# Expert scorer's attention pass: the slots of a step summed on VectorE, with the scan chain and the totals moved some steps back

## The reference, cut to what matters

```python
h = (x_flat @ W_gat).reshape(M, HEADS, NUM_EXPERTS)
a_src = (h * att_src).sum(-1)
a_dst = (h * att_dst).sum(-1)
e = jax.nn.leaky_relu(a_src[src] + a_dst[dst], negative_slope=0.2)
e_max = jax.ops.segment_max(e, dst, num_segments=M)
ee = jnp.exp(e - e_max[dst])
denom = jax.ops.segment_sum(ee, dst, num_segments=M)
alpha = ee / (denom[dst] + 1e-16)
agg = jax.ops.segment_sum(h[src] * alpha[:, :, None], dst, num_segments=M)
```

## Time and profile before

| what | value |
| --- | --- |
| time, median of 3 runs | 12754.23 us (12739.93 to 12757.21) |
| the profiled execution's own time | 12773.27 us |
| its span in the trace | 12771.6 us, granted TensorE clock 0.727 of full |
| PE, DVE, POOL, ACT busy in the span | 7698.0, 6064.4, 6049.9, 2359.1 us |
| the `be` pass, from its first gather to DVE's last instruction | 4396.66 to 5560.40 us |
| its gathers on POOL (L581) | 728, busy 699.4 us, idle before them 451.9 us |

### The profile page before, as it was taken

The page is one execution under the profiler, slowest core; times in us unless marked ns, Lnnn a source line. Parts: engine busy times, 40 slices in busy tenths (PEclk is TensorE's granted clock), DMA queues, the critical chain, the costliest instruction groups (busy, mean ns, idle before and its releaser), DMA issues. The chain is left out here.

```text
span 12771.6 us, 114013 instructions
## 1 busy us (share of the span) xinstructions
PE 7698.0 (60%) x32472; PEld 5982.8 (47%) x32472; DVE 6064.4 (47%) x17050; ACT 2359.1 (18%) x5596; POOL 6049.9 (47%) x6164
## 2 busy tenths in 40 slices
PE   4555464266664478835677575666746746666546
PEld 3334343255553377734566433445535635555334
DVE  6666665388886222232122244655651135444455
ACT  0122010011111144410122011133312211111001
POOL 0666556566662166605666405655521126666000
PEclk9666555577777677767788787777768967777777
DMA  1222122266665111213333602211343323336200
GB/s 46 61 61 64 37 83 63 61 183 183 184 180 92 24 19 19 19 49 90 92 91 92 68 7 50 46 42 43 41 42 105 103 57 96 95 95 90 32 4 22
DMA packets 478286, 903.72 MB, mean 71 GB/s; under 512 B 173139, under 2 KB 290029, under 8 KB 476915
## 3 DMA queue, kind: packets, MB, share of 16 engines
q0 software_dynamic: 277568, 621.62, 22.7%
q1 hardware_dynamic: 200106, 274.86, 6.7%
HBM read 827.17 MB, written 68.88 MB: 70 GB/s over the span
## 5 line engine op out<-in xcount | busy, mean ns | idle before, releaser
L581 POOL DMA_INDIRECT ee_rows<-e_table,net_mr_data x1000 | 998.2, 998 | 1118.9 <-POOLq L1725 466.6
L581 POOL DMA_INDIRECT ge_rows<-g_table,net_mr_data x1000 | 964.1, 964 | 652.1 <-issue 286.0
L913 POOL DMA_INDIRECT ce_rows<-c_table,net_mr_data x1000 | 950.8, 951 | 497.8 <-issue 236.9
L402 POOL DMA_INDIRECT main_slots<-em_load,em_where x784 | 817.2, 1042 | 637.1 <-DVE em_where L376 377.7
L581 POOL DMA_INDIRECT ae_rows<-a_table,net_mr_data x752 | 719.1, 956 | 411.2 <-issue 219.0
L581 POOL DMA_INDIRECT be_rows<-b_table,bx_br_data x728 | 699.4, 961 | 451.9 <-issue 196.3
L627 PE MATMUL ge_to_act<-ge_rows,net_eye 125*125 125x256 f32 x2000 | 636.9, 471 | 179.2 <-issue 172.0
L402 POOL DMA_INDIRECT gat_slots<-eg_load,eg_where x512 | 531.4, 1038 | 380.5 <-DVE eg_where L376 217.4
L627 PE MATMUL ee_to_act<-ee_message,net_eye 125*125 125x256 f32 x2000 | 570.4, 432 | 204.7 <-issue 202.1
L936 PE MATMUL ce_part_ps<-ce_rows,net_eye 125*125 125x256 f32 x2000 | 540.4, 417 | 190.9 <-DMA ce_rows<-c_table,net_mr_data 95.2
L359 PE MATMUL em_look_ps<-em_table,em_hot_tT 25*128 25x125 f32 x1568 | 319.9, 380 | 548.5 <-issue 328.3
(11 more groups left out here) (1006 smaller groups left out, 18294.0 us busy)
## 6 DMA issues: line engine op xcount, KB each, us to landing
em_key_row<-main_keys SPq DMA_DIRECT2D x98, 512.0 KB
f_w<-in_L_ffn_W_dram SPq DMA_DIRECT2D x40, 1024.0 KB, 11.8
eg_key_row<-gat_keys SPq DMA_DIRECT2D x64, 512.0 KB
ce_rows<-c_table,net_mr_data POOLq DMA_INDIRECT x1000
ee_rows<-e_table,net_mr_data POOLq DMA_INDIRECT x1000
ge_rows<-g_table,net_mr_data POOLq DMA_INDIRECT x1000
main_slots<-em_load,em_where POOLq DMA_INDIRECT x784
b_own_rows<-bx_kept SPq DMA_DIRECT2D x100, 125.0 KB
```

The costliest lines, as they stand in the source:

```text
L402: pool.indirect_dma_start(edge["slots"], bass.IndirectOffsetOnAxis(ap=where[:, c:c + 1], axis=0), load[:, c, :], None).then_inc(scattered, 16)
L581: pool.indirect_dma_start(rows[n][:, s, :], None, table, bass.IndirectOffsetOnAxis(ap=data[:, g, s, 0:1].bitcast(I32), axis=0)).then_inc(g ...
L913: pool.indirect_dma_start(rows[:, g % RING, s, :], None, table, bass.IndirectOffsetOnAxis(ap=data[:, g, s, 0:1].bitcast(I32), axis=0)).the ...
```

## The change

A new parameter `late` of `edge_pass`, set in the `be` call alone:

- `sum_slots` and `keep` are gone. In `send`, after a drain, DVE sums the 8 slots itself with one `reduce_sum` over a strided view, 16 sums of 8, written to `part`.
- POOL's wait before a step is on `message_ready` (raised by DVE in `send`) instead of `slot_summed`.
- The block chain and what follows run later: see `AT` in the diff. `total` is now at i-12, `scale` at i-11 and `add` at i-13, so that the loops have 6 more iterations (`END`). `hot` has 20 places and `part` 16.
- PE's order becomes flip, flip_back, own, turn, total, experts. `turn` uses one PSUM bank instead of two, and waits for the copy of the step before. `back_ps` has a bank of its own.
- `lent_part` is a new argument that no call uses.

```diff
-    HOTS, PARTS = 14, 8
+    HOTS, PARTS = (20, 16) if late else (14, 8)
+    AT = dict(flip=4, scan=5, flip_back=7, fall=9, factors=10, scale=11, total=12, lower=12, add=13) if late else dict(flip=3, scan=3, flip_back=4, fall=5, factors=5, scale=6, total=7, lower=6, add=7)
+    END = G + AT["add"] + 1
...
-        to_act = [ps(f"to_act{n}", [128, 512]) for n in range(2)]
+        to_act = [ps(f"to_act{n}", [128, 512]) for n in range(1 if late else 2)]
...
-        topT_ps = back_ps = ps("topT_ps", [128, 512])
+        topT_ps = ps("topT_ps", [128, 512])
+        back_ps = ps("back_ps", [128, 512]) if late else topT_ps
...
-                                pool.wait_ge(slot_summed, g - RING + 1)
+                                pool.wait_ge(message_ready if late else slot_summed, g - RING + 1)
...
                     pe.wait_ge(hot_ready, g + 1)
-                    if g >= 2:
+                    if late and g:
+                        pe.wait_ge(turned_sb, g)
+                    elif g >= 2:
                         pe.wait_ge(turned_sb, g - 1)
...
-                    if 0 <= i - 1 < G:
+                    if 0 <= i - 1 < G and not late:
                         sum_slots(i - 1)
-                    if QW and 0 <= i + 5 < G:
+                    if QW and 0 <= i + 5 < G and not late:
                         turn(i + 5)
                     if QW and 0 <= i + 3 < G:
                         own(i + 3)
+                    if QW and 0 <= i + 5 < G and late:
+                        turn(i + 5)
+                    if 0 <= i - AT["total"] < G and late:
+                        total(i - AT["total"])
...
-                    if 0 <= i - 2 < G:
+                    if 0 <= i - 2 < G and not late:
                         keep(i - 2)
...
+                    if late:
+                        dve.drain()
+                        sums = part[0:NP, g % PARTS, 0:W].rearrange("p (h v) -> p h v", h=H)[:, :, 0:dv]
+                        dve.reduce_sum(sums, values(g).rearrange("p s (h v) -> p h v s", h=H), axis=AX.X)
...
-            edge_pass(nc, edge, table, "add", 4, 4, 20, a_dst, 0.2, acc, const, "be", ring=8, tops=True, inner=inner)
+            edge_pass(nc, edge, table, "add", 4, 4, 20, a_dst, 0.2, acc, const, "be", ring=8, tops=True, inner=inner, late=True)
```

More of the change, by code:

```diff
@@ L499, with edge_pass @@
 BLOCK = 4
-def edge_pass(nc, edge, table, kind, H, dv, row_width, per_target, scores, acc, const, name, ring, more=(), lent=None, lent_whole=None, lent_top=None, tops=False, beside=None, inner=None):
+def edge_pass(nc, edge, table, kind, H, dv, row_width, per_target, scores, acc, const, name, ring, more=(), lent=None, lent_whole=None, lent_top=None, tops=False, beside=None, inner=None, late=False, lent_part=None):
     G, data, ids = edge["G"], edge["data"], edge["tile_of"]
@@ L532, in edge_pass @@
         message = sb("message", [128, 2, SLOTS, VW]) if kind == "mix" else None
-        part = sb("part", [128, PARTS, WA])
+        part = lent_part if lent_part is not None else sb("part", [128, PARTS, WA])
         bounds = lent if lent is not None else sb("bounds", [8, 4 * BLOCK * NP])
@@ L632, in flip @@
                     pe.wait_ge(topped, last + 1)
-                    if b:
+                    if b and late:
+                        pe.wait_ge(scanned, b)
+                    elif b:
                         pe.wait_ge(gap_ready, b)
@@ L642, in flip_back @@
                     pe.wait_ge(spread_ready, b + 1)
+                    if b and late:
+                        pe.wait_ge(gap_ready, b)
+                        pe.wait_ge(lowered, b)
                     for q in range(size[b]):
@@ L653, in total @@
                     ins.then_inc(totalled, 1)
-                for i in range(-5, G + 8):
-                    if 0 <= i - 7 < G:
-                        total(i - 7)
+                for i in range(-5, END):
+                    if 0 <= i - AT["total"] < G and not late:
+                        total(i - AT["total"])
                     for b in range(BLOCKS):
-                        if i == b * BLOCK + 3:
+                        if i == b * BLOCK + AT["flip"]:
                             flip(b)
-                        if i == b * BLOCK + 4:
+                        if i == b * BLOCK + AT["flip_back"]:
                             flip_back(b)
-                    if 0 <= i - 1 < G:
+                    if 0 <= i - 1 < G and not late:
                         sum_slots(i - 1)
-                    if QW and 0 <= i + 5 < G:
+                    if QW and 0 <= i + 5 < G and not late:
                         turn(i + 5)
@@ L684, in turned_copy @@
                     act.wait_ge(turned, g + 1)
-                    if 0 <= g - 6 < G:
+                    if 0 <= g - 6 < G and not late:
                         act.wait_ge(slot_summed, g - 5)
@@ L708, in factors @@
                         act.wait_ge(scaled, (b - 1) * BLOCK)
+                    if late and b * BLOCK + size[b] > PARTS:
+                        act.wait_ge(totalled, b * BLOCK + size[b] - PARTS)
                     if tops:
@@ L714, in factors @@
                     act.activation(fall[0:NP, b % 2, :], back_ps[0:NP, 64:64 + H], ACT.Exp).then_inc(lowered, 1)
-                for i in range(-6, G + 8):
+                for i in range(-6, END):
                     if 0 <= i + 1 < G:
@@ L821, in scale @@
                     dve.wait_ge(factor_ready, b + 1)
-                    dve.wait_ge(part_kept, g + 1)
+                    if not late:
+                        dve.wait_ge(part_kept, g + 1)
                     p = part[0:NP, g % PARTS, 0:W].rearrange("p (h v) -> p h v", h=H)
@@ L832, in _ @@
                 dve.memset(low[:, :], -FAR)
-                for i in range(-4, G + 8):
+                for i in range(-4, END):
                     if 0 <= i + 1 < G:
```

19 lines of the change are left out of this document (11 added, 8 removed).

## The result

The kernel after takes 12927.83 us (median of 4 runs, 12898.01 to 12929.96), the kernel before 12755.72 us (4 runs, 12739.93 to 12759.54). The ratio is 1.0132, with a 95% interval of 1.0114 to 1.0149: slower by 172 us. The prediction had the sign, and a third of the size (+55 us); the time lies above its range (12680 to 12890).

The account below looks back on a forecast made before the run. The bound was taken to be POOL's 10.0 us of gathers a step and their drain, with PE's signals late meanwhile. Steps +47, start -12 and end +20 made +55 us on 12754: 12809 us, range 12680 to 12890.

Parts of the forecast that it names:

- PE's work taken out is worth nothing: In `be`, leaving out PE records of 201.1 us, 2.2 a step, gains nothing, hidden by POOL and its drain.
- DVE's sum: In DVE's `send`, 0.3 us plus 0.1 for the drain a step, hidden; 36 us at most if uncovered.
- The start: Start of the `be` pass: step 8 may begin after DVE's message of step 0, 12 us earlier.
- POOL's wait: POOL's wait in `be`, moved from PE to DVE: steps of 12.3 instead of 11.73 us, +47 us over 82 steps.
- the forecast: The main case for `be`: steps of 11.9 to 13.5 us, 12776 to 12907 us; chance 0.47.
- The single bank: `turn` on PE waits for the copy of the step before, taken as made an iteration earlier: costs nothing.
- The end: From step 90 to the end of `be`: 117 us instead of 96, with 8 messages left, +20 us.
- The six added iterations: End of the `be` pass: six more iterations with only total, scale and add, 1 us each, 6 us.
- the signals come through: Rival: with DVE's gate PE's signals arrive freely, POOL takes 10.0 us a step; about -182, 12572 us; chance 0.17.
- The lock stays: Rival: POOL still pauses for the drain alone, 11.5 to 11.73 us a step; 12743 to 12762 us; chance 0.23.
- A mild gain: Rival: steps of 11.3 us in `be` or a shorter end, down to 12700 us; chance 0.10.
- DVE becomes the bound: Rival: DVE's added work in `be` is uncovered, 36 us, 12790 us; chance 0.03.

Follow-up runs that it names:

- both: Kernel after with `turn` behind the experts' matmuls and POOL waiting for PE again; 0.9985 and 1.0012 of before with pauses, 1.0014 on the chip without.
- turn_last_half: Kernel after with `turn` behind the experts' matmuls and POOL allowed 4 steps ahead instead of 8; 13031.63 us, 1.0147 of before.
- turn_last: Kernel after with `turn` behind the experts' matmuls, single bank kept; 12954.84 us, 1.0127 of before; on the chip without pauses 11660.33 us, 1.0012.
- pe_gate: Kernel after with POOL waiting for PE again, single bank kept; 12812.21 us, 1.0027 of before; on the chip without pauses 11715.87 us, 1.0058.
- before_one_bank: Kernel before with `turn` waiting for the previous step's copy, as with one bank; 1.0137 on the chip without pauses, 1.0070 on one with.
- the silent runs: Kernels before, after, and after with `turn` behind the experts' matmuls, without gathers past the first 8 steps; PE's ring 7.05, 10.32, 6.71 us a unit.

## Why the prediction was half right

- **What bounds the kernel** (PE's signals are late while POOL gathers, POOL's run and its silence make the step) held on every chip like that of the result. That it would not hold on all chips was not foreseen: on one of the five the signals are not late.
- **PE's work taken out is worth nothing:** right. "both" has all of it taken out, and DVE's sum in, and stands at 0.9985, 1.0012 and 1.0014.
- **DVE's sum:** 374 ns where I took 300. It is hidden, as said. By the Trainium skill ("VectorE: DVE Perf Modes", The TRN2 errata) it would be the 0.19 us estimated ahead, by a cost of which the same section says that it comes out too low for a single operation; the row has twice that.
- **The start:** step 8 begins 11.6 us earlier; predicted 12.
- **POOL's wait** (the gate): the mechanism is right, and it is the cause. With it undone alone, 1.0127 falls to 1.0027. The step that failed is the size of its term in the sum, "The ring of 8 is deeper than that of `ee` (5 places), so I take the row of 24 and the one of 64 as neighbours, and about 12.3". The length of a run isn't set by the ring's depth: turn_last_half has half of it and the same runs. It is set by how many messages PE's chain gets through, one in the silence and one soon behind it, and so no run without a stop of more than 0.3 us is longer than 16. The formula, (20 + 3 + 4.5) / 2 = 13.7 for runs of 16, stood in the prediction and met the measured 13.93 and 14.06 us of turn_last; it was fed the wrong length. Measured in the kernel after: 13.51 us, and +146 us over 82 steps instead of +47. That is just outside the 11.9 to 13.5 of the forecast, whose own range went to 12907 while the one stated stopped at 12890. The silence is put at "about 0.2 us a gather"; the three rows behind it give 0.21, 0.14 and 0.16, and the 2.75 us after 16 gathers 0.17.
- **The single bank, "nothing":** wrong as a price, and of little weight for this result. I had taken the copy as made an iteration earlier. It is made in the same one, behind Gelu and Exp on ACT's queue, and PE's ring goes from 7.05 to 10.32 us. With DVE's gate in place, the middle of the pass doesn't feel it: turn_last's steps are longer, not shorter. The end does: there the 8 messages that are left took 77 us (L806 starts at 5593.45 and 5670.56, the first five gaps between are 10.5 to 12.2 us) instead of the 64.5 predicted, and 58 in turn_last. The longer steps and the shorter end together leave turn_last at 12955 us, beside 12930. The six added iterations took 6.9 us from the last of the experts' results to the last add; predicted 6.
- **The rivals:** *the signals come through* is false where the result was measured and true on the one chip without pauses. There "both" and turn_last have steps of 10.1 us, but the kernel before is as fast (11645 us, 14 and 16 us less than the two), and the -182 us are not to be had. The Trainium skill's rule ("TensorE: Matmul & The Clock Gate", The cost: per-tile semaphore tail), some 26 ns for an increment, is nearer to the 0.08 us of that chip than to the others, where the signals wait up to 10 us behind the last gather. *The lock stays* is false for the kernel after, and is what pe_gate and "both" bring back. *A mild gain* and *DVE becomes the bound* are false: DVE is busy for 201.18 of 800 us.

**What stays open.** What holds PE's signals up, and why on most chips and not on one. It may be more than a signal: in the kernel before, while POOL issues its first 64 gathers, the four matmuls of one `own` (L617), with nothing but weight loads between them, come with wide gaps for which the profile names no wait (in the middle of the pass, at 4906.86, four of them take 0.85 us together):

```profile
4425.55 0.17 PE L617 MATMUL be_own_ps<-b_a_dst,be_hotT 125*125 x1
4426.21 0.17 PE L617 MATMUL be_own_ps<-b_a_dst,be_hotT 125*125 x1 [0.48 <-issue]
4429.01 0.17 PE L617 MATMUL be_own_ps<-b_a_dst,be_hotT 125*125 x1 [2.63 <-issue]
4431.11 0.17 PE L617 MATMUL be_own_ps<-b_a_dst,be_hotT 125*125 x1 [1.93 <-issue]
```

The chips differ in the gathers' transfers too. From 4450 to 4950 us the DMA engines are busy for a share of 0.49 in both2, on the chip without pauses, and of 0.15 in both3, at 22 and 18 GB/s; and DVE waits for gathered rows 91 times, 546.9 us in all, in both2, and once, 12.7 us, in both3. No run tells whether that is a cause or a consequence. Open is also what the kernel after costs on the chip without pauses: it never met it. before_one_bank (1.0137) and the silent runs (10.32 us against POOL's 10.0) let one expect a loss there too, from the bank; that is argued and not shown.

## What to carry to other kernels

Before you move a wait from a late signal to an early one, ask what the waiting engine's pauses were good for: here POOL's stop for PE was what let PE's signals through, and a gate on a third engine that is opened sooner made every cycle longer. Such a finding can hold on one chip and not on the next, so repeat the run on several before you settle on a mechanism. Size a stall that repeats itself by following one cycle to its end, each signal in turn, instead of by the depth of the buffer; the depth is only a limit. Where two buffers are made one, write down for each user of it what stands ahead on its engine's queue: the wait was on a copy of 0.35 us, the price was the Gelu and the Exp ahead of it, and with POOL silent an order with `turn` last paid nothing.

## What the runs showed of the hardware

- The same kernel takes 11645 us on one chip and 12777 to 12853 us on others. The difference is in POOL's idle time. For "both" on the first (both2) and on another (both3) the spans are 11654.2 and 12770.2 us, 1116 apart; POOL's idle time in its seven largest groups of indirect DMAs adds to 3060.6 and 4162.5 us, 1102 apart, and their busy time differs by 10. In this pass the idle time in front of the 728 gathers is 295.9 and 448.9 us, of which the wait for the pass to begin is 74.4 and 74.5.
- The mean duration of a gather is nearly the same on both (957 and 950 ns), and so is the gap of 0.30 us to the next. It is PE's signals that come late.
- An optimisation can be settled by the one mechanism on one chip and by another on the next: undoing the bank was worth 0.4% on the first (pe_gate to "both") and, in the kernel after, nothing on one of the others (after and turn_last, both 1.0127); undoing the gate was worth nothing on the first (turn_last to "both", 1.0012 and 1.0014) and 1.0% on that other (after to pe_gate).
